# The gate's clamp reads its exponential from PSUM, and four small pieces of the sequence stage change places

## The chip, the cores and the metric

One Trainium2 chip, one of its cores. The metric is the device time of one execution in microseconds (us). The kernel before took 900.95 us, the median of 3 runs (900.33 to 901.28).

## The reference, cut to what matters

32 sequences of 512 tokens with 256 channels each go through an RWKV time-mixing layer with a residual and a layer norm; a second layer then works on a few selected tokens. Only the first layer is touched:

```python
k, v, r = (einsum('btc,oc->bto', x * mix + shifted(x) * (1 - mix), W) for Wk, Wv, Wr)
sr = sigmoid(r)
# per channel, over t:  out = (a + exp(u + k) * v) / (b + exp(u + k))
#                       a = a * ew + exp(k) * v;  b = b * ew + exp(k)
x = layernorm(x + einsum('btc,oc->bto', sr * out, Wo))      # over the 256 channels
```

The second layer (router, top 64 tokens of each pair of half-lengths, attention among them, a feed-forward block, a layer norm) follows when all 32 sequences are through.

## The kernel before, in words

**Tiling.** A sequence is held with its channels on the 128 partitions, in two halves of 512 tokens: a tile of one sequence is 128x1024. The stage over the sequences is a software pipeline written out by hand: each engine has a function `period(at)` that lists what it does in period n, for sequence n and for its neighbours, and `periods` (L367) runs it for 32 periods and DEPTH more, so that the last sequences drain. Nothing else orders the work: each engine executes its list in order and waits on semaphores.

**What each engine does in period n**, in its order:

- TensorE (L640): the three projections of n, K, V and R (L623, 24 matmul instructions in the trace, 8 for each), then the output projection of n-1 with the residual added by a transpose (L635, L637). K waits for `den_done`, V for `num_done` and R for `er_done` of n-1, since those release the PSUM banks.
- ScalarE, ACT in the rows (L932): two exponentials of K of n, one to SBUF and one in place in PSUM (L884, L886); the reciprocal of n-1 as an exponential (L907, waits for `sum_done`); the scaling of the differences of n+1 (L915, three instructions); the exponential of -R (L892, PSUM to the SBUF tile `er`); the logarithm of the denominator (L898, waits for `den_done`); the logarithm of the gate (L902, waits for `clamp_done`); the evacuation of the output of n-1 from PSUM (L923); the rows of n-3, that is the scaling by the layer norm's statistics, four instructions (L928, waits for `nm_done`).
- VectorE, DVE in the rows (L1186): the scan of the denominator of n (L1129, waits for the second exponential of K); the denominator (L1143); the product with V (L1136, in PSUM); the clamp of the gate's exponential to 2^62 (L1149, waits for `er_done`, SBUF to SBUF); the scan of the numerator and the numerator (L1154, L1159); the small shift of n-3 (L1183, 128x4, waits for `s2_done`) and a copy of its statistics (L1184, 128x28); the statistics of n-2: four bn_stats (L1166), four dot products with the router's weights (L1171, a custom instruction with two SBUF inputs of 128x256), four aggregates (L1174) and two small instructions of 128x4 (L1178, L1179).
- GpSimd, POOL in the rows (L558): the difference of n+1 (L525); the gate of n-1, numerator by reciprocal (L547, waits for `rec_done`; its end releases the output projection); three mixes of n+1 (L531, wait for `scaled`); the power for the statistics of n-3 (L554); the sum of the two logarithms of n (L538, waits for `ls_done`).
- SyncE (L468): the loads of sequence n+2 (L456, L457 after `mixed` of n-2 and L461 after `y_ready` of n-2), then the store of n-4 (L466, waits for `rows_done`).

**Buffers.** `er`, `ld`, `den`, `num`, `gg`, `st6`, `stat` and `nm` have two copies each, `xc` and `xt` a ring of four. The PSUM banks of K, V, R and of the output have one copy each.

```python
def statistics_of(s):                       # two SBUF inputs: xt and rwb
    ...
        v.tensor_tensor_reduce(junk[:, j, :], xt[s.k][:, j, :], rwb[:, :], 1.0, 0.0, ALU.mult, ALU.add,
                               stat[par][:, j, 2:3])
```

Of the kernel before, what the change touches and what calls it, by code (L numbers as in the profile page):

```python
# [7 lines left out]
def rwkv_then_selected_block_kernel(nc, x_chan, w_attn, columns, mask_rows, positions,  # L8
# [16 lines left out]
    ALU = mybir.AluOpType  # L25
    ACT = mybir.ActivationFunctionType
# [8 lines left out]
    RING = 4  # L35
# [22 lines left out]
    with ctx:  # L58
# [57 lines left out]
        er = both(CC, T)  # L116
# [31 lines left out]
        psK, psV, psR = ps[:, 0:2, :], ps[:, 2:4, :], ps[:, 4:6, :]  # L148
# [87 lines left out]
        k_ready = sem("k_ready")  # L236
        v_ready = sem("v_ready")
        r_ready = sem("r_ready")
# [5 lines left out]
        er_done = sem("er_done")  # L244
        clamp_done = sem("clamp_done")
# [116 lines left out]

        block = ctx.enter_context(nc.Block())

        DEPTH = 3

        def periods(eng, period):  # L367

# [74 lines left out]
        @block.sync  # L443
        def _(sp):
            sp.dma_start(cols[:, :], columns).then_inc(small_in, 16)
            sp.dma_start(rwb[:, :], router_w.rearrange("(a c) -> a c", a=1).to_broadcast([P, C])).then_inc(small_in, 16)
            sp.dma_start(rbb[:, :], router_b.rearrange("(a c) -> a c", a=1).to_broadcast([P, 1])).then_inc(small_in, 16)

            def load_channels(s):
                if s.had(RING):  # L450

                    sp.wait_ge(mixed, s.n - (RING - 1))
                else:

                    sp.wait_ge(edges_zero, 2 * RING)
                sp.dma_start(xs[s.k][0:HALF, 1:T], x_chan[s.n, 0:HALF, 0:T - 1]).then_inc(chan_in[s.k], 16)  # L456
                sp.dma_start(xs[s.k][HALF:P, 0:T - 1], x_chan[s.n, HALF:P, 1:T]).then_inc(chan_in[s.k], 16)  # L457
                if s.had(RING):

                    sp.wait_ge(y_ready, s.n - (RING - 1))  # L460
                sp.dma_start(xc[s.k][:, :, :], chan_v[s.n]).then_inc(chan_in[s.k], 16)  # L461

            def store_rows(s):

                sp.wait_ge(rows_done, s.n + 1)
                sp.dma_start(out_v[s.n], xt[s.k][:, :, :]).then_inc(row_out[s.k], 16)  # L466

            def period(at):  # L468
                if at.back(-2).exists():
                    load_channels(at.back(-2))  # L470
                if at.had(4) and at.back(4).exists():
                    store_rows(at.back(4))

            load_channels(At(0, 0))
            sp.dma_start(wa[:, :, :, :], w_attn.rearrange("m (c p) o -> p m c o", p=P)).then_inc(w_in, 16)
            load_channels(At(0, 1))
            for k in range(RING):
                period(At(0, k))
            sp.dma_start(ptok[:, :, :], positions.rearrange("p (b j) -> p b j", b=MB)).then_inc(pos_in, 16)
            for dst, src in ((wqk, w_qk), (wv, w_v), (wo, w_o)):  # L480
                sp.dma_start(dst[:, :, :], src.rearrange("(c p) o -> p c o", p=P)).then_inc(w2_in, 16)
            with sp.Fori(1, B // RING - 1) as i:
                for k in range(RING):
                    period(At(i, k))
            for k in range(RING + DEPTH + 1):
                period(At(B // RING - 1, k))

            sp.wait_ge(mall_done, NP)
            sp.wait_ge(ssq_done, NP)
            sp.dma_start(w_stage.rearrange("p (c o) -> p c o", o=F), w_up.rearrange("(c p) o -> p c o", p=P)).then_inc(w_staged, 16)  # L490
            sp.wait_ge(w_split, 1)
            sp.dma_start(w_stage.rearrange("p (c o) -> p c o", o=C), w_down.rearrange("(c p) o -> p c o", p=P)).then_inc(w_staged, 16)
# [113 lines left out]
        def _(pe):  # L606
# [6 lines left out]

            def projections(s):
                pe.wait_ge(mixed, s.n + 1)
                for m, bank, ready, used in ((0, psK, k_ready, den_done), (1, psV, v_ready, num_done), (2, psR, r_ready, er_done)):
                    if s.had(1):

                        pe.wait_ge(used, s.n)
                    for o in range(CC):  # L620
                        for c in range(CC):
                            rhs = xm[s.par][:, m, :] if c == 0 else xc[s.k][:, c, :]
                            last = mm(bank[:, o, :], wa[:, m, c, o * P:(o + 1) * P], rhs, start=(c == 0), stop=(c == CC - 1))  # L623
                    last.then_inc(ready, 1)
# [248 lines left out]
        def _(act):  # L873
            a = nc.scalar
# [12 lines left out]

            def exp_r_of(s):
                act.wait_ge(r_ready, s.n + 1)
                if s.had(2):  # L890
                    act.wait_ge(sum_done, s.n - 1)
                a.activation(er[s.par][:, :, :], psR[:, :, :], ACT.Exp, scale=-1.0).then_inc(er_done, 1)  # L892

            def ln_den_of(s):
                act.wait_ge(den_done, s.n + 1)
                if s.had(2):
                    act.wait_ge(g_ready, s.n - 1)
                a.activation(ld[s.par][:, :, :], den[s.par][:, :, :], ACT.Ln, scale=2.0 ** -DEN_EXP).then_inc(ld_done, 1)  # L898

            def ln_gate_of(s):  # L900
                act.wait_ge(clamp_done, s.n + 1)
                a.activation(er[s.par][:, :, :], er[s.par][:, :, :], ACT.Ln, bias=1.0).then_inc(ls_done, 1)  # L902

            def reciprocal_of(s):

                act.wait_ge(sum_done, s.n + 1)
                a.activation(ld[s.par][:, :, :], ld[s.par][:, :, :], ACT.Exp, scale=-1.0, bias=lnbias[:, 0:1]).then_inc(rec_done, 1)  # L907
# [17 lines left out]
            def rows_of(s):  # L925
                act.wait_ge(nm_done, s.n + 1)
                for j in range(TJ):
                    last = a.activation(xt[s.k][:, j, :], xt[s.k][:, j, :], ACT.Identity,  # L928
                                        scale=stat[s.par][:, j, S2:S2 + 1], bias=nm[s.par][:, j:j + 1])
                last.then_inc(rows_done, 1)  # L930

            def period(at):  # L932
                if at.exists():
                    exp_k_of(at)
                if at.had(1) and at.back(1).exists():
                    reciprocal_of(at.back(1))
                if at.back(-1).exists():
                    differences_scaled(at.back(-1))
                if at.exists():
                    exp_r_of(at)  # L940
                    ln_den_of(at)
                    ln_gate_of(at)
                if at.had(1) and at.back(1).exists():
                    evacuation_of(at.back(1))
                if at.had(3) and at.back(3).exists():
                    rows_of(at.back(3))

            periods(act, period)

# [133 lines left out]
        def _(dve):  # L1083
# [62 lines left out]
            def clamp_of(s):  # L1146

                dve.wait_ge(er_done, s.n + 1)
                v.tensor_scalar(er[s.par][:, :, :], er[s.par][:, :, :], 2.0 ** 62, None, ALU.min).then_inc(clamp_done, 1)  # L1149

            def num_of(s):
                dve.wait_ge(ekv_done, s.n + 1)
# [9 lines left out]
            def statistics_of(s):  # L1162
                par = s.par
                dve.wait_ge(y_read, s.n + 1)
                for j in range(TJ):
                    last = v.bn_stats(st6[par][:, j, :], xt[s.k][:, j, :])  # L1166
                last.then_inc(bn_done, 1)
                for j in range(TJ):
                    if j == TJ - 1:
                        dve.wait_ge(bn_done, s.n + 1)  # L1170
                    v.tensor_tensor_reduce(junk[:, j, :], xt[s.k][:, j, :], rwb[:, :], 1.0, 0.0, ALU.mult, ALU.add,  # L1171
                                           stat[par][:, j, 2:3])
                for j in range(TJ):
                    last = v.bn_aggr(stat[par][:, j, 0:2], st6[par][:, j, :])  # L1174
                last.then_inc(aggr_done, 1)
                dve.wait_ge(aggr_done, s.n + 1)

                v.tensor_scalar(stat[par][:, :, VE], stat[par][:, :, VAR], EPS, None, ALU.add)  # L1178
                v.tensor_scalar(stat[par][:, :, VN], stat[par][:, :, VAR], 1.0 + EPS / 4, EPS * EPS / 4, ALU.mult, ALU.add).then_inc(t2_done, 1)  # L1179
# [6 lines left out]
            def period(at):  # L1186
                if at.exists():
                    den_scan_of(at)
                    den_of(at)
                    products_of(at)  # L1190
                    clamp_of(at)
                    num_of(at)
                if at.had(3) and at.back(3).exists():
                    shift_of(at.back(3))
                if at.had(2) and at.back(2).exists():
                    statistics_of(at.back(2))

            periods(dve, period)

# [290 lines left out]
```

## Time and profile before

| | |
|---|---|
| median of 3 runs | 900.95 us |
| the profiled execution | 907.34 us |
| its span, first to last instruction | 905.6 us |
| granted TensorE clock, mean | 0.942 |
| busy: PE, DVE, ACT, POOL | 779.3, 729.3, 496.5, 437.3 us |
| idle of PE before L635, behind POOL's gate L547 | 27.3 us |
| idle of ACT before its rows L928, behind DVE's shift L1183 | 67.8 us |
| idle of DVE before its scan L1129, behind ACT's L886 | 27.5 us |

The profile shows one execution. A row of the timeline begins with the start and the duration in us, then engine, line, operation, tiles and shapes; "x3" is the number of instructions merged in it, and a bracket gives the idle time of the engine before it and what ended it. Rows of one line give the shortest, the median and the longest duration in ns. Instructions of DVE, ACT and POOL overlap their predecessor a little, so that the step from one start to the next is some 0.04 to 0.1 us shorter than the duration. An instruction that waits for a resource after its start has the wait in its duration.

### The profile page before, as it was taken

How to read it: one execution, taken by the hardware profiler on the slowest of the kernel's cores; microseconds unless marked ns; L12 is line 12 of the kernel's file. 1: busy time of each engine (PE TensorE's matmuls, PEld its weight loads, DVE VectorE, ACT ScalarE, POOL GpSimd, SP SyncE). 2: the span in 40 equal slices, each digit the busy share in tenths (PEclk: the TensorE clock that was granted, in tenths of full speed). 3: DMA queues.
4: the chain of work that ended last, by engine and by line, in shares of the span. 5: the costliest groups of instructions: out<-in, count | busy, mean ns of one | idle time of the engine just before them, and what ended most of it. 6: DMA issues, size and time to landing. Idle time of an engine off the chain costs nothing. (4 is left out here: it accounts for less than half of the span.)

```text
span 905.6 us, 12959 instructions
## 1 busy us (share of the span) xinstructions
PE 779.3 (86%) x4228; PEld 522.4 (58%) x4228; DVE 729.3 (81%) x1505; ACT 496.5 (55%) x825; POOL 437.3 (48%) x303
## 2 busy tenths in 40 slices
PE   7999999999999999999999607397788888799983
PEld 4455554545555554545455405395566666699983
DVE  4689999999999999999999788446777787347773
ACT  2566757676676767676676421063567676431210
POOL 1667686868677786868686505444100000001223
PEclk9999999999999999999999855598999999999996
DMA  7122222231322223221310122342000000000000
GB/s 203 35 82 82 93 82 93 73 100 58 96 78 81 93 81 93 81 93 59 103 58 29 42 70 58 105 117 93 1 2 1 0 1 2 2 1 13 23 24 35
DMA packets 37317, 55.14 MB, mean 61 GB/s; under 512 B 3360, under 2 KB 26528, under 8 KB 37280
## 3 DMA queue, kind: packets, MB, share of 16 engines
q1 hardware_dynamic: 34464, 46.28, 16.4%
q0 software_dynamic: 2816, 8.39, 3.1%
q8 instruction: 21, 0.34, 0.2%
q14 instruction: 16, 0.13, 0.0%
HBM read 35.78 MB, written 18.87 MB: 60 GB/s over the span
## 5 line engine op out<-in xcount | busy, mean ns | idle before, releaser
L623 PE MATMUL ps<-arena,wa 128*128 128x512 f32 x768 | 337.0, 595 | 6.0 <-DMA wa<-w_attn 4.3
L623 PEld LDWEIGHTS ps<-arena,wa 128*128 128x128 f32 x768 | 146.2, 191 | 178.4 <-issue 169.0
L547 POOL TENSOR_TENSOR arena<-arena 128x1024 f32<-128x1024 f32 x32 | 75.5, 2360 | 123.5 <-issue 70.2
L637 PE MATMUL ps<-wa,arena 128*128 128x256 f32 x512 | 133.3, 383 | 0.0
L531 POOL TENSOR_TENSOR arena<-arena 128x512 f32<-128x512 f32 x93 | 128.1, 1407 | 4.6 <-ACT arena L915 4.6
L599 POOL TENSOR_TENSOR fst<-fst,mhalf 128x2 f32<-128x2 f32 x8 | 5.8, 720 | 235.8 <-DVE fst L1448 235.8
L928 ACT ACTIVATE arena<-arena 128x256 f32<-128x256 f32 x128 | 66.3, 590 | 67.8 <-DVE arena L1183 67.8
L1129 DVE TENSOR_TENSOR_SCAN arena<-ewb,ps 128x511 f32<-128x511 f32 x64 | 74.5, 1205 | 27.6 <-ACT ps L886 27.5
L637 PEld LDWEIGHTS ps<-wa,arena 128*128 128x128 f32 x512 | 88.4, 193 | 6.8
L538 POOL TENSOR_TENSOR arena<-arena 128x1024 f32<-128x1024 f32 x32 | 75.1, 2348 | 7.1 <-ACT arena L902 7.1
L635 PE MATMUL ps<-ident,arena 128*128 128x128 f32 x256 | 51.0, 281 | 27.3 <-POOL arena L547 27.3
L1154 DVE TENSOR_TENSOR_SCAN arena<-ewb,ps 128x511 f32<-128x511 f32 x64 | 74.0, 1195 | 0.0
L635 PEld LDWEIGHTS ps<-ident,arena 128*128 128x128 f32 x256 | 34.1, 143 | 62.2 <-POOL arena L547 41.4
L915 ACT ACTIVATE arena<-arena,cols 128x512 f32<-128x512 f32 x93 | 60.0, 710 | 0.0
L902 ACT ACTIVATE arena<-arena 128x1024 f32<-128x1024 f32 x32 | 33.8, 1057 | 46.5 <-DVE arena L1149 46.5
L554 POOL TENSOR_TENSOR arena<-arena,mhalf 128x8 f32<-128x8 f32 x32 | 53.7, 1679 | 7.8 <-DVE arena L1179 7.8
L1149 DVE TENSOR_SCALAR arena<-arena 128x1024 f32<-128x1024 f32 x32 | 51.0, 1594 | 5.0 <-ACT arena L892 4.9
L1078 ACT ACTIVATE arena<-ps 128x512 f32<-128x512 f32 x32 | 19.1, 598 | 61.1 <-PE ps L848 61.1
L859 PE MATMUL ps<-halves 128*128 128x256 f32 x384 | 48.9, 288 | 3.7 <-DVE halves L1419 3.7
L1183 DVE SCALAR_TENSOR_TENSOR arena<-arena 128x4 f32<-128x4 f32 x32 | 44.9, 1402 | 7.4 <-POOL arena L554 7.4
L859 PEld LDWEIGHTS ps<-halves 128*128 128x128 f32 x384 | 48.1, 197 | 3.9 <-DVE halves L1419 3.9
L923 ACT ACTIVATE arena<-ps 128x1024 f32<-128x1024 f32 x32 | 32.7, 1023 | 28.8 <-PE ps L637 28.8
(179 smaller groups left out, 1431.7 us busy)
## 6 DMA issues: line engine op xcount, KB each, us to landing
arena<-x_chan SPq DMA_DIRECT2D x32, 512.0 KB, 3.5
out<-arena SPq DMA_DIRECT2D x32, 512.0 KB, 3.3
arena<-x_chan SPq DMA_DIRECT2D x64, 127.8 KB, 3.2
wa<-w_attn SPq DMA_DIRECT2D x1, 1024.0 KB, 7.9
arena<-w_up SPq DMA_DIRECT2D x1, 1024.0 KB, 4.8
arena<-w_down SPq DMA_DIRECT2D x1, 1024.0 KB, 5.6
wqk<-w_qk SPq DMA_DIRECT2D x1, 512.0 KB, 4.6
wv<-w_v SPq DMA_DIRECT2D x1, 256.0 KB, 5.3
```

Source lines behind the costliest of these rows:

```text
L531: last = g.tensor_tensor(xm[s.par][:, m, :], xm[s.par][:, m, :], xs[s.k][:, :], ALU.add)
L538: g.tensor_tensor(ld[s.par][:, :, :], ld[s.par][:, :, :], er[s.par][:, :, :], ALU.add).then_inc(sum_done, 1)
L547: g.tensor_tensor(gg[s.par][:, :, :], num[s.par][:, :, :], ld[s.par][:, :, :], ALU.mult).then_inc(g_ready, 1)
L554: g.tensor_tensor(stat[s.par][:, :, S1:S2 + 1], stat[s.par][:, :, VE:VN + 1], mhalf[:, 0:2 * TJ].rearrange("p (j a) -> p j a", a=2), ALU.p ...
L623: last = mm(bank[:, o, :], wa[:, m, c, o * P:(o + 1) * P], rhs, start=(c == 0), stop=(c == CC - 1))
L635: mm(psY[:, j, c * P:(c + 1) * P], xc[s.k][:, c, tokens], ident[:, :], is_transpose=True, start=(c == 0), stop=False)
L637: last = mm(psY[:, j, :], gg[s.par][:, c, tokens], wa[:, 3, c, :], start=False, stop=(c == CC - 1))
L859: last = mm(ps[:, 4 + g.par, i * C:(i + 1) * C], x[:, f, i * P:(i + 1) * P], w[:, f, :], start=(f == 0 and t == 0), stop=(f == FC - 1 and ...
L915: last = a.activation(xm[s.par][:, m, :], diff[:, :], ACT.Copy, scale=mix[:, m:m + 1])
L928: last = a.activation(xt[s.k][:, j, :], xt[s.k][:, j, :], ACT.Identity, scale=stat[s.par][:, j, S2:S2 + 1], bias=nm[s.par][:, j:j + 1])
L1129: last = v.tensor_tensor_scan(bb[:, c, 1:T], ewb[:, c, 0:T - 1], psK[:, c, 0:T - 1], 0.0, ALU.mult, ALU.add)
L1154: v.tensor_tensor_scan(aa[:, c, 1:T], ewb[:, c, 0:T - 1], psV[:, c, 0:T - 1], 0.0, ALU.mult, ALU.add).then_inc(scan_a_done, 1)
```

## The change

DEPTH goes from 3 to 4, so every engine has one draining period more; SyncE's list stays as long as it was. ScalarE writes the exponential of -R back to the PSUM bank of R in place of `er`; the clamp reads it there and writes `er`, and now holds the wait on `sum_done` that protects `er`. The R projection of the next sequence waits for `clamp_done` in place of `er_done`. On ScalarE the reciprocal of n-1 comes first in the period, and the rows are those of n-4, between the logarithm of the denominator and that of the gate. On VectorE the small shift and its copy come behind the statistics. The statistics wait for `stats_kept` of two sequences before.

```diff
-        DEPTH = 3
+        DEPTH = 4
...
-            for k in range(RING + DEPTH + 1):
+            for k in range(RING + DEPTH):
                 period(At(B // RING - 1, k))
...
-                for m, bank, ready, used in ((0, psK, k_ready, den_done), (1, psV, v_ready, num_done), (2, psR, r_ready, er_done)):
+                for m, bank, ready, used in ((0, psK, k_ready, den_done), (1, psV, v_ready, num_done), (2, psR, r_ready, clamp_done)):
...
             def exp_r_of(s):
                 act.wait_ge(r_ready, s.n + 1)
-                if s.had(2):
-                    act.wait_ge(sum_done, s.n - 1)
-                a.activation(er[s.par][:, :, :], psR[:, :, :], ACT.Exp, scale=-1.0).then_inc(er_done, 1)
+                a.activation(psR[:, :, :], psR[:, :, :], ACT.Exp, scale=-1.0).then_inc(er_done, 1)
...
             def period(at):
+                if at.had(1) and at.back(1).exists():
+                    reciprocal_of(at.back(1))
                 if at.exists():
                     exp_k_of(at)
-                if at.had(1) and at.back(1).exists():
-                    reciprocal_of(at.back(1))
                 if at.back(-1).exists():
                     differences_scaled(at.back(-1))
                 if at.exists():
                     exp_r_of(at)
                     ln_den_of(at)
+                if at.had(4) and at.back(4).exists():
+                    rows_of(at.back(4))
+                if at.exists():
                     ln_gate_of(at)
                 if at.had(1) and at.back(1).exists():
                     evacuation_of(at.back(1))
-                if at.had(3) and at.back(3).exists():
-                    rows_of(at.back(3))
...
                 dve.wait_ge(er_done, s.n + 1)
-                v.tensor_scalar(er[s.par][:, :, :], er[s.par][:, :, :], 2.0 ** 62, None, ALU.min).then_inc(clamp_done, 1)
+                if s.had(2):
+                    dve.wait_ge(sum_done, s.n - 1)
+                v.tensor_scalar(er[s.par][:, :, :], psR[:, :, :], 2.0 ** 62, None, ALU.min).then_inc(clamp_done, 1)
...
                 dve.wait_ge(y_read, s.n + 1)
+                if s.had(2):
+                    dve.wait_ge(stats_kept, s.n - 1)
...
                     num_of(at)
+                if at.had(2) and at.back(2).exists():
+                    statistics_of(at.back(2))
                 if at.had(3) and at.back(3).exists():
                     shift_of(at.back(3))
-                if at.had(2) and at.back(2).exists():
-                    statistics_of(at.back(2))
```

## Rows read from the trace of the kernel before

**Rows 1.** The page's slices: granted TensorE clock in tenths, 40 slices of the span.
```profile
PEclk9999999999999999999999855598999999999996
```

**Rows 2.** Timeline, PE: the begin of an output projection.
```profile
424.32 0.44 PE L635 MATMUL ps<-ident,arena 128*128 128x128 f32 x2 [0.73 <-POOL arena L547]
```

**Rows 3.** Timeline, DVE and ACT: one round of the closed chain.
```profile
420.74 2.33 DVE L1129 TENSOR_TENSOR_SCAN arena<-ewb,ps 128x511 f32<-128x511 f32 x2 [0.62 <-ACT ps L886]
...
423.17 1.41 DVE L1143 SCALAR_TENSOR_TENSOR arena<-ps,euw,arena 128x512 f32<-128x512 f32 x2
...
425.62 1.65 DVE L1149 TENSOR_SCALAR arena<-arena 128x1024 f32<-128x1024 f32 x1
...
427.20 2.31 DVE L1154 TENSOR_TENSOR_SCAN arena<-ewb,ps 128x511 f32<-128x511 f32 x2
...
430.73 1.62 DVE L1183 SCALAR_TENSOR_TENSOR arena<-arena 128x4 f32<-128x4 f32 x1
...
432.39 2.08 ACT L928 ACTIVATE arena<-arena 128x256 f32<-128x256 f32 x4 [2.46 <-DVE arena L1183]
...
434.38 1.00 ACT L884 ACTIVATE arena<-ps 128x1024 f32<-128x1024 f32 x1
...
436.32 2.33 DVE L1129 TENSOR_TENSOR_SCAN arena<-ewb,ps 128x511 f32<-128x511 f32 x2 [0.62 <-ACT ps L886]
```

**Rows 4.** Timeline, the other steps of the same sequences on ACT and POOL.
```profile
421.91 2.36 POOL L547 TENSOR_TENSOR arena<-arena 128x1024 f32<-128x1024 f32 x1 [3.91 <-issue]
...
424.61 1.06 ACT L898 ACTIVATE arena<-arena 128x1024 f32<-128x1024 f32 x1
...
429.99 2.35 POOL L538 TENSOR_TENSOR arena<-arena 128x1024 f32<-128x1024 f32 x1
...
436.22 1.13 ACT L907 ACTIVATE arena<-arena,lnbias 128x1024 f32<-128x1024 f32 x1
...
437.25 1.94 ACT L915 ACTIVATE arena<-arena,cols 128x512 f32<-128x512 f32 x3
```

**Rows 5.** Timeline, PE: projections of the fourth, the fifth and the last sequence.
```profile
55.61 10.46 PE L623 MATMUL ps<-arena,wa 128*128 128x512 f32 x24
...
70.25 10.46 PE L623 MATMUL ps<-arena,wa 128*128 128x512 f32 x24
...
491.04 10.46 PE L623 MATMUL ps<-arena,wa 128*128 128x512 f32 x24
```

**Rows 6.** By line, POOL's mixes: durations in ns, shortest/median/longest.
```profile
L531 POOL TENSOR_TENSOR arena<-arena x93: 1257/1281/1743, 21.4 to 489.0; 128x512 f32<-128x512 f32 x93
```

**Rows 7.** Timeline: the copy behind the shift and POOL's difference, started together.
```profile
244.75 1.31 DVE L1184 COPY stats_all<-arena 128x28 f32 x1
...
244.75 1.28 POOL L525 TENSOR_TENSOR arena<-arena 128x512 f32<-128x512 f32 x1
```

**Rows 8.** Timeline, second layer: two DVE instructions, two SBUF inputs each, beside POOL.
```profile
619.38 5.95 DVE L1365 TENSOR_TENSOR arena<-arena 128x256 f32<-128x256 f32 x2
...
620.48 4.57 POOL L596 TENSOR_TENSOR halves<-arena,halves 128x2048 fp32r<-128x2048 f32 x1
```

**Rows 9.** By line and timeline, DVE: the dot products and their neighbours.
```profile
L1171 DVE CUSTOM_DVE_ANT_0 arena<-arena,rwb x128: 398/415/422, 59.1 to 523.5; 128x256 f32<-128x256 f32 x128
...
401.12 1.39 DVE L1166 BATCH_NORM_STATS2 arena<-arena 128x6 f32<-128x256 f32 x4
...
402.43 0.40 DVE L1171 CUSTOM_DVE_ANT_0 arena<-arena,rwb 128x256 f32<-128x256 f32 x1
...
404.21 0.17 DVE L1178 TENSOR_SCALAR arena<-arena 128x4 f32<-128x4 f32 x1
```

**Rows 10.** By line, DVE: the product in PSUM, the clamp, the shift.
```profile
L1136 DVE TENSOR_TENSOR ps<-arena,ps x32: 1217/1219/1221, 23.3 to 502.4; 128x1024 f32<-128x1024 f32 x32
...
L1149 DVE TENSOR_SCALAR arena<-arena x32: 686/1670/1817, 25.4 to 503.5; 128x1024 f32<-128x1024 f32 x32
...
L1183 DVE SCALAR_TENSOR_TENSOR arena<-arena x32: 154/1620/1627, 72.4 to 526.2; 128x4 f32<-128x4 f32 x32
```

## The prediction

> **What bounds the kernel now.** I read the slices first, then the timeline of one period in the middle of the sequence stage, then the waits, then the pairs of rows in which VectorE and GpSimd run side by side. The granted clock is at its full 2.4 GHz through the sequence stage [rows 1], so the durations of PE hold for all of it. From the fifth to the last sequence a period takes (491.04 - 70.25) / 27 = 15.58 us [rows 5]. TensorE is nearly full, yet it does not set that length: it waits 0.73 us in each period for the gate [rows 2], and where it does not wait a period is 70.25 - 55.61 = 14.64 us [rows 5]. What sets it is a closed chain of DVE and ACT: scan of the denominator 2.43, denominator and product 2.45, clamp 1.58, scan of the numerator and numerator 3.53, small shift to the rows 1.66, rows to the first exponential 1.99, the two exponentials 1.94, and then the next scan: 15.58 us from start to start [rows 3], the period itself. In that chain both the rows on ACT and the shift on DVE are in line.
>
> Two of its links are long for another reason. The shift of 128x4 takes 154 ns at best and 1620 at the median [rows 10]; it starts at 430.73 and ends at 432.35, when POOL's sum ends (429.99 + 2.35) [rows 3, 4]. The clamp takes 686 ns at best and 1670 at the median [rows 10], beside POOL's mixes, whose own longest is 1743 against a median of 1281 [rows 6]. So a DVE instruction of such a kind waits for the POOL instruction in flight, and holds up the next one. The copy of 128x28 does too: once it started together with POOL's difference and took 1.31 us [rows 7]. Two instructions with two SBUF inputs, one after the other, took 5.95 us from 619.38, to 0.28 us after the end of a POOL instruction of 4.57 us that had started at 620.48 [rows 8]: the second was let in only when that one was over. A waiting DVE instruction gets one turn between two of POOL's, not a run of turns.
>
> **The change part by part.**
>
> *Clamp from PSUM.* No row shows a tensor_scalar of 1024 elements from PSUM. The nearest on the one side is the clamp undisturbed, 0.69 us, on the other the product in PSUM, 1.22 [rows 10]. I take 1.2, since that row too reads 1024 elements from PSUM. Having no second SBUF side, it should no longer wait for the mixes nor delay them: start to start 1.1 in place of 1.58, 0.5 us less on DVE. The exponential written to PSUM costs the same as one to SBUF: ACT's exponential of K writes either, 1.0 us each (the two take 1.94 [rows 3]). The R bank is released later, by the clamp, but R is projected 7.0 us (two thirds of 10.46 [rows 5]) into the period, long after: nothing.
>
> *Shift behind the statistics, rows a sequence later.* It takes shift, rows and exponentials out of line: rows(n-4) find their shift done. Off the old chain go 1.66 + 1.99. On ACT the 1.98 us of rows now stand between the logarithm of the denominator and that of the gate, so gate, sum, reciprocal and gate product come behind them.
>
> *Reciprocal first.* It starts when the sum is over, and no longer behind 1.94 us of exponentials; the exponentials then come 1.0 us behind it.
>
> *The rest.* The store of n-4 is issued behind rows that are done in the middle of the period; behind it on SyncE wait the loads of n+3, needed over a period later, so their cover is some 15 us. The ring of four `xt` still leaves about a period between rows and the next evacuation. The three new waits (stats_kept, and sum_done at the clamp, both two sequences back, and clamp_done) are met long before; behind the clamp's wait on DVE stand the numerator and the statistics. The draining period has no new work. I put 0 on all of this, and 2 us to either side for the drain.
>
> *What the dots meet.* This is the point that decides. Before, the four dots fell into the 3.91 us in which POOL stood idle ahead of its gate [rows 4]; all 128 took 398 to 422 ns [rows 9], so the trace never shows one against POOL. They read two SBUF tensors, as the shift and the pair in [rows 8] do. Cost beside POOL: from 0 (they are a custom instruction and might be free of it) to a whole POOL instruction each. I take the latter. Now the clamp's end is followed by 3.5 us of numerator [rows 3] and 1.3 of bn_stats [rows 9], then the dots; and on POOL the sum 2.35, the difference 1.28 and the gate 2.36 go off one behind the other, since the reciprocal is ready at once. The dots fall among them: one passes after the difference, the second waits out the gate.
>
> Then another chain closes, from the end of the gate to the end of the next. Three dots, aggregates and the two small instructions: four dots and aggregates take 404.21 - 402.43 = 1.78 [rows 9], so 1.4 for three, less 0.1 of overlap; 1.3. The first small tensor_scalar meets the mixes, which start 1.0 + 1.9 + 1.9 + 0.1 = 5.0 us after the start of the reciprocal (that, two exponentials, scaling [rows 3, 4]), the gate 1.3 us after it; so the gate's end is at 3.7 and the mixes begin at 1.3 us behind that, just when it asks. It waits a mix, 1.2; the shift, 0.2 behind it, waits most of the next, 1.1; copy 0.1: den scan at 1.3 + 1.2 + 1.3 = 3.8 us. Scan and denominator 2.43 + 1.41 = 3.85 [rows 3]. ACT: logarithm 1.0, rows 2.0, logarithm 1.06, hand-over 0.1 [rows 3, 4]: 4.15. Sum 2.35, reciprocal 1.13, hand-overs 0.2, gate 2.36 plus 0.1 behind the dot [rows 4]: 6.15. Together 3.8 + 3.85 + 4.15 + 6.15 = 17.95 us in place of 15.58: 2.35 more. PE, at 14.64, then idles some 3.3 us, of which most before V, which waits for the numerator. Here the reordering costs: 2 us of rows stand in the chain, and it contains every POOL step but the mixes.
>
> About 25 periods run at that length (the first six have no dots, or have not drifted yet): 25 x 2.35 = 59 us. On the profiled execution, span 905.6, time 907.34: 966. The profiled execution lies 6.4 us above the median of the runs; carried over to that: 900.95 + 59 = 960 us.
>
> The Trainium skill, SBUF — State Buffer, "Who interferes with whom", says that a Vector instruction with two SBUF inputs contends with a GpSimd instruction that reads SBUF, and that copies and tensor_scalar in a mode that uses both ports do so as well. By that rule the dots and the small tensor_scalar would both wait; the trace agrees for the shift (1620 ns against 154 [rows 10]), and shows no dot beside POOL.
>
> **The rivals.**
>
> *A shorter stall: the small tensor_scalar are free.* If only dots, shift and copy wait, the shift waits the rest of the first mix, 0.9 and no more: the den scan comes at 2.55, the chain is 16.7 us, 25 x 1.1 = 27 us: 928. For it: the race with the mix is a matter of 0.1 us, and no row shows an instruction of 128x4 with one input beside POOL. Against it: clamp and copy, of the same kinds, both wait.
>
> *A longer one.* Where the copy loses its turn as well, as once in 32 [rows 7], a period is 19.1: 25 x 3.5 = 88, 989. I think it rare.
>
> *The other side: the dots do not contend.* Then DVE has 2.43 + 2.45 + 1.1 + 3.53 + 1.3 + 1.78 + 0.2 + 0.2 = 13.0 us of work, and the chain from the denominator's scan through both logarithms, rows, sum, reciprocal and exponentials back to it is 3.85 + 4.15 + 2.4 + 1.1 + 1.95 = 13.45: PE sets the period. 26 x (15.58 - 14.64) = 24, and 1 to 3 us more as the last gate comes earlier: 875. For it: it removes both links that wait now, and the custom instruction is unseen beside POOL. Against: its input count, and the pair in [rows 8]. It decides at the point where a dot beside POOL costs under some 0.4 us.
>
> *No change.* The old rate returns if the dots wait for one POOL instruction in all: 15.6 us, 901.
>
> **How the numbers follow.** 17.95 us a period has 0.36, 16.7 has 0.32, 19.1 has 0.08; the dots free 0.19; no change 0.05. The predicted time is that of the first, 960. The slower cases run from 928 (less 10 for a later onset and the clamp's lower bound, so 915) to 989: that is 0.76; down to 901 takes in no change: 0.81. The range is 900 to 990 and leaves out the dots free. Faster or slower count from 0.2%, 1.8 us, about what a measurement of this kernel can tell from no change: 0.19 faster, 0.05 the same, 0.76 slower.
>
> **What would show it.** Right: the dots' longest at 2 us or more in place of 422 ns; the first small tensor_scalar at 1.2 us; the clamp at a steady 1.2, mixes at 1.28; PE idle before its projections behind DVE's numerator; a period near 18 us. Dots at 0.4 us beside POOL and a period of 14.64 would make it wrong on the other side; tensor_scalar at 0.17 with dots that wait give 16.7. If the clamp still swings with the mixes, my first term is wrong.

## The result, and the profile after

The changed kernel takes 957.19 us, the median of 4 runs (954.4 to 959.73), against 900.64 us for the one before: a ratio of 1.063, 95% interval 1.0588 to 1.0672. It is slower by 6.3%; the forecast was 960 us.

The page of the changed kernel, part 2 (TensorE's busy tenths and its granted clock) and part 5 (groups by line; behind the bar the busy time, the mean of one in ns, and the engine's idle time ahead of them with what ended most of it):

```profile
PE   7999888888889888888888861688688889799983
...
PEclk9999999999999999999999976559799999999996
...
L623 PE MATMUL ps<-arena,wa 128*128 128x512 f32 x768 | 355.3, 615 | 66.7 <-DVE arena L1160 49.2
...
L1174 DVE CUSTOM_DVE_ANT_0 arena<-arena,rwb 128x256 f32<-128x256 f32 x128 | 126.6, 1041 | 0.0
...
L896 ACT ACTIVATE arena<-arena 128x1024 f32<-128x1024 f32 x32 | 33.8, 1056 | 89.5 <-DVE arena L1142 89.5
...
L926 ACT ACTIVATE arena<-arena 128x256 f32<-128x256 f32 x128 | 65.9, 586 | 5.1 <-DVE arena L1186 5.1
```

In these tenths the clock of the sequence stage is as before [rows 1]. Taken period by period it is not quite: in 6 of the last 25 periods TensorE's clock falls to its lower level, 1.2 GHz, for some 3 us (granted clock 0.50 from 124.60 to 127.10, 0.91 over that period), where the kernel before has 1.00 in every one. It costs no more than the last period's 0.9 us: a period with such a fall takes 18.7 us and the one behind it 16.9, together two of 17.8, and e8 below has the same period without one fall. The time lies in the waits. TensorE now waits 66.7 us ahead of its projections, 49.2 of them for VectorE's numerator (L1160). The wait of ACT's rows for the shift, 67.8 us in the table of before, is 5.1: the change did cut that link. In its place the dot products, 0.41 us each before, take 1.04 on average.

PE's timeline in the changed kernel gives the period. A row of 24 matmul instructions holds the projections of K, V and R; where V waits, the 8 of K stand apart. The row at 123.47 is V and R with a fall of the clock in it:

```profile
85.30 10.46 PE L623 MATMUL ps<-arena,wa 128*128 128x512 f32 x24
...
99.98 3.67 PE L623 MATMUL ps<-arena,wa 128*128 128x512 f32 x8
105.69 7.13 PE L623 MATMUL ps<-arena,wa 128*128 128x512 f32 x16 [2.03 <-DVE arena L1160]
...
117.77 3.67 PE L623 MATMUL ps<-arena,wa 128*128 128x512 f32 x8 [0.61 <-DVE arena L1142]
123.47 8.83 PE L623 MATMUL ps<-arena,wa 128*128 128x512 f32 x16 [2.03 <-DVE arena L1160]
...
545.92 3.60 PE L623 MATMUL ps<-arena,wa 128*128 128x512 f32 x8
```

From 85.30 to 99.98 PE still sets the period, 14.68 us. Then comes a step to 17.79, and from 99.98 to the last sequence 25 periods take (545.92 - 99.98) / 25 = 17.84 us, against 15.58 [rows 5]. That is 25 x 2.26 = 56 us, as much as the medians are apart. The two traces say nearly the same: the last sequence begins 545.92 - 491.04 = 54.9 us later.

The new closed chain, called the ring below, runs from the end of one gate to the end of the next. One round of it, from the timeline of DVE, ACT and POOL in the changed kernel:

```profile
410.30 2.41 POOL L547 TENSOR_TENSOR arena<-arena 128x1024 f32<-128x1024 f32 x1
...
410.44 2.56 DVE L1174 CUSTOM_DVE_ANT_0 arena<-arena,rwb 128x256 f32<-128x256 f32 x1
...
413.93 3.73 POOL L531 TENSOR_TENSOR arena<-arena 128x512 f32<-128x512 f32 x3 [1.22 <-ACT arena L913]
414.02 1.20 DVE L1181 TENSOR_SCALAR arena<-arena 128x4 f32<-128x4 f32 x1
...
415.21 1.23 DVE L1186 SCALAR_TENSOR_TENSOR arena<-arena 128x4 f32<-128x4 f32 x1
...
416.45 2.31 DVE L1128 TENSOR_TENSOR_SCAN arena<-ewb,ps 128x511 f32<-128x511 f32 x2
...
418.87 1.41 DVE L1142 SCALAR_TENSOR_TENSOR arena<-ps,euw,arena 128x512 f32<-128x512 f32 x2
...
420.31 1.06 ACT L896 ACTIVATE arena<-arena 128x1024 f32<-128x1024 f32 x1 [3.79 <-DVE arena L1142]
...
421.27 2.06 ACT L926 ACTIVATE arena<-arena 128x256 f32<-128x256 f32 x4
...
423.24 1.04 ACT L900 ACTIVATE arena<-arena 128x1024 f32<-128x1024 f32 x1
...
424.42 2.35 POOL L538 TENSOR_TENSOR arena<-arena 128x1024 f32<-128x1024 f32 x1 [5.15 <-ACT arena L900]
...
426.73 1.27 POOL L525 TENSOR_TENSOR arena<-arena 128x512 f32<-128x512 f32 x1
...
427.30 0.99 DVE L1174 CUSTOM_DVE_ANT_0 arena<-arena,rwb 128x256 f32<-128x256 f32 x1
...
428.18 2.35 POOL L547 TENSOR_TENSOR arena<-arena 128x1024 f32<-128x1024 f32 x1 [0.18 <-ACT arena L905]
```

The gate ends at 412.71, and the second dot, started at 410.44, ends 0.29 us behind it. The first small tensor_scalar starts 0.09 us behind the first mix and lasts 1.20; the shift lasts 1.23 beside the second mix. The scan of the denominator follows 3.74 us behind the gate's end. From there it is 3.86 us to the logarithm of the denominator (L896), 4.11 us with the rows and the logarithm of the gate (L900) to the sum, and 6.11 us to the end of the next gate (430.53): 17.82 us. The first dot of the next round (427.30) lasts 0.99: it ends 0.29 us behind POOL's difference, which ends at 428.00.

By line, the clamp, the first small tensor_scalar and the mixes of the changed kernel (shortest/median/longest in ns):

```profile
L1150 DVE TENSOR_SCALAR arena<-ps x32: 1215/1217/1225, 25.3 to 561.0; 128x1024 f32<-128x1024 f32 x32
...
L1181 DVE TENSOR_SCALAR arena<-arena x32: 171/1178/1203, 62.8 to 581.3; 128x4 f32<-128x4 f32 x32
...
L531 POOL TENSOR_TENSOR arena<-arena x93: 1260/1267/1284, 21.3 to 541.0; 128x512 f32<-128x512 f32 x93
```

### The profile page after: what moved, and what is told of

Its sections match the earlier page's. It is cut to its first block and busy times, and to the rows that moved or that the text cites. A ratio compares the mean times of both kernels' runs of the same rounds, so it can differ in the third digit from the quotient of the medians.

```text
span 958.0 us, 12995 instructions
## 1 busy us (share of the span) xinstructions
PE 796.7 (83%) x4228; PEld 527.0 (55%) x4228; DVE 810.4 (85%) x1505; ACT 492.9 (51%) x825; POOL 427.2 (45%) x303
## 3 DMA queue, kind: packets, MB, share of 16 engines
q1 hardware_dynamic: 34464, 46.28, 15.8%
## 5 line engine op out<-in xcount | busy, mean ns | idle before, releaser
L623 PE MATMUL ps<-arena,wa 128*128 128x512 f32 x768 | 355.3, 615 | 66.7 <-DVE arena L1160 49.2
L531 POOL TENSOR_TENSOR arena<-arena 128x512 f32<-128x512 f32 x93 | 115.5, 1269 | 42.8 <-ACT arena L913 42.8
L1174 DVE CUSTOM_DVE_ANT_0 arena<-arena,rwb 128x256 f32<-128x256 f32 x128 | 126.6, 1041 | 0.0
L896 ACT ACTIVATE arena<-arena 128x1024 f32<-128x1024 f32 x32 | 33.8, 1056 | 89.5 <-DVE arena L1142 89.5
L890 ACT ACTIVATE ps<-ps 128x1024 f32<-128x1024 f32 x32 | 32.3, 1008 | 71.7 <-PE ps L623 71.7
L905 ACT ACTIVATE arena<-arena,lnbias 128x1024 f32<-128x1024 f32 x32 | 36.8, 1149 | 49.8 <-POOL arena L538 49.8
L554 POOL TENSOR_TENSOR arena<-arena,mhalf 128x8 f32<-128x8 f32 x32 | 52.7, 1648 | 9.0 <-DVE arena L1182 9.0
L635 PEld LDWEIGHTS ps<-ident,arena 128*128 128x128 f32 x256 | 36.5, 143 | 34.9 <-issue 16.7
L859 PEld LDWEIGHTS ps<-halves 128*128 128x128 f32 x384 | 49.2, 202 | 3.9 <-DVE halves L1422 3.9
```

The source lines that it names most:

```text
L531: last = g.tensor_tensor(xm[s.par][:, m, :], xm[s.par][:, m, :], xs[s.k][:, :], ALU.add)
L635: mm(psY[:, j, c * P:(c + 1) * P], xc[s.k][:, c, tokens], ident[:, :], is_transpose=True, start=(c == 0), stop=False)
L859: last = mm(ps[:, 4 + g.par, i * C:(i + 1) * C], x[:, f, i * P:(i + 1) * P], w[:, f, :], start=(f == 0 and t == 0), stop=(f == FC - 1 and ...
```

## The experiments

Two theories stood against each other. **A**: the ring is closed by VectorE's instructions that wait out POOL's, above all the dots behind the gate. **B**: only the work put in line counts (2 us of rows between the two logarithms); waits beside POOL don't matter. The kernels are called e1 to e10. The first four kernels and the ninth and tenth ran where the kernel before takes 901 us; the fifth to the eighth where it takes 910.92, so the ratio to before is what compares.

| kernel | median us | before | ratio, 95% interval |
|---|---|---|---|
| the changed kernel | 957.19 | 900.64 | 1.063 (1.0588 to 1.0672) |
| e1 changed, reciprocal back | 876.32 | 901.2 | 0.9726 (0.9682 to 0.9769) |
| e2 changed, rows at the end | 918.12 | 901.2 | 1.0189 (1.0146 to 1.0233) |
| e3 changed, shift first | 925.55 | 901.2 | 1.0272 (1.0209 to 1.0334) |
| e4 changed, dots with one input | 875.65 | 901.2 | 0.9718 (0.9679 to 0.9758) |
| e5 before, rows later | 891.49 | 910.92 | 0.9789 (0.9738 to 0.9839) |
| e6 before, clamp from PSUM | 902.05 | 910.92 | 0.9899 (0.9843 to 0.9956) |
| e7 before, reciprocal first | 898.09 | 910.92 | 0.9861 (0.9832 to 0.989) |
| e8 changed, clamp in SBUF | 969.23 | 910.92 | 1.0642 (1.0611 to 1.0673) |
| e9 changed, small instructions as memsets | 926.03 | 901.56 | 1.0273 (1.0252 to 1.0294) |
| e10 as e1, three rounds | 874.13 | 901.56 | 0.9707 (0.9683 to 0.9732) |

### The reciprocal put back

```diff
             def period(at):
-                if at.had(1) and at.back(1).exists():
-                    reciprocal_of(at.back(1))
                 if at.exists():
                     exp_k_of(at)
+                if at.had(1) and at.back(1).exists():
+                    reciprocal_of(at.back(1))
```

> The changed kernel with the reciprocal put back behind the two exponentials of K; all else as changed. Theory A (a ring closed by the dots that wait out POOL's gate): the gate now starts some 1.9 us later after the sum, so the four dots, the small instructions and the shift find POOL with only its difference to do and pass before the gate; the ring opens and PE sets the period at 14.64 us, 25 to 27 periods x 3.15 us less than the 957 us of the changed kernel: about 875 us, dots at 0.4 us (one of four up to 1 us). Theory B (the length is only that of the work put in line, the 2 us of rows between the two logarithms; no wait for a port matters): the rows still stand there and nothing gets shorter, 955 to 960 us.

Measured: 876.32 us, the ratio 0.9726. A holds, B does not: the same work on every engine, with one instruction 1.9 us later, takes 81 us less than the changed kernel. PE's timeline of this kernel:

```profile
394.08 10.46 PE L623 MATMUL ps<-arena,wa 128*128 128x512 f32 x24
...
408.72 10.46 PE L623 MATMUL ps<-arena,wa 128*128 128x512 f32 x24
```

The period is 14.64 us, the one without waits [rows 5]. And what the dots meet, on DVE and POOL:

```profile
426.24 0.63 DVE L1174 CUSTOM_DVE_ANT_0 arena<-arena,rwb 128x256 f32<-128x256 f32 x1
...
426.54 1.46 POOL L525 TENSOR_TENSOR arena<-arena 128x512 f32<-128x512 f32 x1
...
426.81 1.48 DVE L1174 CUSTOM_DVE_ANT_0 arena<-arena,rwb 128x256 f32<-128x256 f32 x1
...
429.54 0.17 DVE L1187 COPY stats_all<-arena 128x28 f32 x1
...
430.11 2.37 POOL L547 TENSOR_TENSOR arena<-arena 128x1024 f32<-128x1024 f32 x1 [2.11 <-issue]
```

The dots still wait, for the end of the sum and for the difference, but all of them and the copy behind them (429.54) are through before the gate begins at 430.11.

### The dots with one input

```diff
-                    v.tensor_tensor_reduce(junk[:, j, :], xt[s.k][:, j, :], rwb[:, :], 1.0, 0.0, ALU.mult, ALU.add,
-                                           stat[par][:, j, 2:3])
+                    v.bn_stats(junk[:, j, 0:6], xt[s.k][:, j, :])
```

> The changed kernel with each of the four dot products replaced by a bn_stats of the same 128x256 (one SBUF input, 0.33 us in place of 0.35), so that VectorE has the same work but none of the four takes a second SBUF input; the dot product with the router's weights is left out and the selection goes by the mean in its place. Theory A: without the dots' wait the ring is not closed, the small instructions come long before the mixes, and PE sets the period: 14.64 us, about 875 us. Theory B: the same work in the same places, 957 us.

Measured: 875.65 us. By line, the durations in ns (shortest/median/longest) of the four replacements in this kernel:

```profile
L1176 DVE BATCH_NORM_STATS2 arena<-arena x128: 405/409/416, 58.9 to 496.9; 128x6 f32<-128x256 f32 x128
```

and of the dots in the changed kernel:

```profile
L1174 DVE CUSTOM_DVE_ANT_0 arena<-arena,rwb x128: 405/418/2595, 58.9 to 580.5; 128x256 f32<-128x256 f32 x128
```

The reciprocal is still first and the rows are still between the logarithms; only the four dots are replaced, and the whole loss is gone. This is the direct test of the step that decides: the loss hangs on the dots and their waits for POOL. That a dot waits because of its second SBUF input is not separated here, since bn_stats is another operation and writes 6 elements in place of 256 as well. The Trainium skill (SBUF — State Buffer, "Who interferes with whom") says that a Vector instruction with two SBUF inputs contends with a GpSimd instruction that reads SBUF. The trace agrees for the dots: 0.41 us alone, up to 2.6 behind a gate.

One wait did not go. The first small tensor_scalar of this kernel now asks during the gate and waits that out, longer than in the changed kernel:

```profile
412.26 1.93 DVE L1182 TENSOR_SCALAR arena<-arena 128x4 f32<-128x4 f32 x1
...
414.34 2.31 DVE L1130 TENSOR_TENSOR_SCAN arena<-ewb,ps 128x511 f32<-128x511 f32 x2
```

POOL's gate ends at 414.16, and the scan starts 0.18 us behind it, where 3.74 us lay between the two in the changed kernel. So, by an estimate from the legs of the changed kernel, a ring of 17.82 - 3.74 + 0.18 = 14.3 us is left. That is under TensorE's 14.64, and the wait costs nothing.

### The other moves undone, one at a time

The rows at the end of ACT's period:

```diff
-                if at.had(4) and at.back(4).exists():
-                    rows_of(at.back(4))
-                if at.exists():
                     ln_gate_of(at)
                 if at.had(1) and at.back(1).exists():
                     evacuation_of(at.back(1))
+                if at.had(4) and at.back(4).exists():
+                    rows_of(at.back(4))
```

> The changed kernel with the rows (still those of four sequences back) at the end of ACT's period. Theory A: the ring loses 1.98 us of rows but the dots still wait out the gate; the small instructions then meet the mixes at another point; worked through step by step a period of about 16.3 us, 957 - 25 x 1.5 = about 918 us (910 to 925), with dots still up to 2.5 us. Theory B: the 2 us of rows go fully, 25 x 2 = 50 us less, 907 us, and with nothing else in line the period falls on towards 14.64 (875).

Measured: 918.12 us, and a period of 422.40 - 406.23 = 16.17 us in PE's timeline:

```profile
406.23 3.60 PE L623 MATMUL ps<-arena,wa 128*128 128x512 f32 x8
411.10 7.13 PE L623 MATMUL ps<-arena,wa 128*128 128x512 f32 x16 [1.27 <-DVE arena L1159]
...
422.40 3.60 PE L623 MATMUL ps<-arena,wa 128*128 128x512 f32 x8
```

The ring loses 1.65 us and stays closed: its dots last up to 2.58 us. B, by which the period had to fall to 15.8 or below, falls here too. But the 1.65 us do not come from the moved rows alone. Four lines of one round:

```profile
405.36 1.06 ACT L896 ACTIVATE arena<-arena 128x1024 f32<-128x1024 f32 x1 [2.25 <-DVE arena L1141]
...
407.54 1.06 ACT L900 ACTIVATE arena<-arena 128x1024 f32<-128x1024 f32 x1 [1.13 <-DVE arena L1149]
...
412.73 2.50 POOL L547 TENSOR_TENSOR arena<-arena 128x1024 f32<-128x1024 f32 x1 [0.40 <-ACT arena L905]
...
416.19 0.17 DVE L1180 TENSOR_SCALAR arena<-arena 128x4 f32<-128x4 f32 x1
```

With nothing between the two logarithms, the logarithm of the gate waits 1.13 us for the clamp (L1149), so logarithm to sum (408.74) takes 3.38 us in place of 4.11: only 0.73 less. The leg from the gate's end to the scan (415.23 to 417.59) is 1.38 shorter: one dot fewer is left behind the gate, and the first small tensor_scalar therefore comes just ahead of the first mix and lasts 0.17. The other two legs are 0.08 and 0.38 longer.

The shift first:

```diff
+                if at.had(3) and at.back(3).exists():
+                    shift_of(at.back(3))
                 if at.had(2) and at.back(2).exists():
                     statistics_of(at.back(2))
-                if at.had(3) and at.back(3).exists():
-                    shift_of(at.back(3))
```

> The changed kernel with the small shift and its copy put back ahead of the statistics. Theory A: the shift waits out a part of the sum again, but no longer behind the dots, where it met the second mix; the ring through gate and dots loses that one wait: about 16.7 us a period, 957 - 25 x 1.1 = about 929 us. Theory B: the shift is not in line with anything after the change, no difference: 957 us.

Measured: 925.55 us. The placing of the shift behind the statistics alone costs 957.19 - 925.55 = 32 us, 1.3 us in each of 25 periods. Shift and copy stand for 1.24 us of the ring above (415.21 to 416.45), nearly all of it the shift's wait for a mix.

The two small instructions as memsets:

```diff
-                v.tensor_scalar(stat[par][:, :, VE], stat[par][:, :, VAR], EPS, None, ALU.add)
-                v.tensor_scalar(stat[par][:, :, VN], stat[par][:, :, VAR], 1.0 + EPS / 4, EPS * EPS / 4, ALU.mult, ALU.add).then_inc(t2_done, 1)
+                v.memset(stat[par][:, :, VE], 1.0)
+                v.memset(stat[par][:, :, VN], 1.0).then_inc(t2_done, 1)
```

> The changed kernel with the two small tensor_scalar of 128x4 behind the aggregates replaced by memsets of the same 128x4, which read nothing from SBUF; the variance is left out of the layer norm's scale (a constant stands there). Theory A (each of the waits counts by itself): the first small instruction no longer waits 1.2 us for the first mix; the shift takes that wait over, 0.9 to 1.1 us, and the second mix is met by nobody: 16.7 us a period, ratio to before about 1.03, 928 us. Rival (all the waits of the ring fall to the dots and the shift alone): no difference, ratio 1.063, 957 us.

Measured: 926.03 us, ratio 1.0273, and 430.43 - 413.88 = 16.55 us a period in PE's timeline:

```profile
413.88 3.60 PE L623 MATMUL ps<-arena,wa 128*128 128x512 f32 x8
419.12 7.13 PE L623 MATMUL ps<-arena,wa 128*128 128x512 f32 x16 [1.65 <-DVE arena L1160]
...
430.43 3.60 PE L623 MATMUL ps<-arena,wa 128*128 128x512 f32 x8
```

This is the case of the prediction's first rival, brought about: with small instructions that are free of POOL the ring is 16.7 us long by its count and 16.55 by the trace. So the wait of a 128x4 tensor_scalar is a term of its own, worth 31 us.

The clamp in SBUF again (the exponential of R to `er`, as before):

```diff
-                a.activation(psR[:, :, :], psR[:, :, :], ACT.Exp, scale=-1.0).then_inc(er_done, 1)
+                if s.had(2):
+                    act.wait_ge(sum_done, s.n - 1)
+                a.activation(er[s.par][:, :, :], psR[:, :, :], ACT.Exp, scale=-1.0).then_inc(er_done, 1)
...
-                v.tensor_scalar(er[s.par][:, :, :], psR[:, :, :], 2.0 ** 62, None, ALU.min).then_inc(clamp_done, 1)
+                v.tensor_scalar(er[s.par][:, :, :], er[s.par][:, :, :], 2.0 ** 62, None, ALU.min).then_inc(clamp_done, 1)
```

> The changed kernel with the clamp part undone (exponential of R to SBUF, clamp there). Theory A: the clamp is not in the new ring (it comes behind the denominator, beside ACT's logarithm and rows), so the period stays near 17.8 us: 955 to 958 us. If the clamp's place or the later release of the R bank mattered, the time would fall by 25 x 0.5 us or more, to 945 us or under.

Measured: ratio 1.0642 against 1.063: no difference. The clamp itself went from a steady 1.22 us to 0.69 us, since in the new order it comes when POOL stands idle:

```profile
L1150 DVE TENSOR_SCALAR arena<-arena x32: 684/686/1064, 26.4 to 559.5; 128x1024 f32<-128x1024 f32 x32
```

So in the new order reading PSUM makes the clamp dearer by half a microsecond. That costs nothing, for the clamp is not in the ring there. TensorE's clock stays at its upper level through all the periods of e8, which take 17.80 us, so the falls of the clock in the changed kernel do not make its period.

### Each part alone, on the kernel before

Rows a sequence later, at their old place:

```diff
-        DEPTH = 3
+        DEPTH = 4
...
-                if at.had(3) and at.back(3).exists():
-                    rows_of(at.back(3))
+                if at.had(4) and at.back(4).exists():
+                    rows_of(at.back(4))
```

> The kernel before with one part of the change alone: the rows are those of four sequences back, at the same place at the end of ACT's period (DEPTH 4). Theory A: the chain shift, rows, exponentials, scan that set the 15.58 us is cut, since the rows no longer wait for this period's shift; the gate comes behind the exponentials, so the dots keep their gap on POOL: PE sets the period at 14.64 us, about 877 us. Theory B (work in line on ACT is what counts): the rows still stand ahead of the exponentials, same time, 900 us.

Measured: ratio 0.9789, where 877 us would be 0.973, just under the interval; the period is 14.64 us as expected:

```profile
406.35 10.46 PE L623 MATMUL ps<-arena,wa 128*128 128x512 f32 x24
...
420.99 10.46 PE L623 MATMUL ps<-arena,wa 128*128 128x512 f32 x24
```

The old chain is cut by this one part. Some 4 us of the expected gain are missing, and they do not lie in the sequence stage: its last sequence starts at 464.90, 26.1 us earlier than in the trace of before (491.04). Behind that start e5 takes 423.0 us, e6, e7 and e8 421.0 to 423.4, the trace of before 414.6 and e1 408.0. So all four traces from that chip are slower in this part; no profile of the kernel before was taken there, and the two runs of e5 are 3.7 us apart, so the 4 us stay open. The clamp still lasts 1.8 us beside the mixes, and it costs nothing now.

The clamp from PSUM alone (the edit above, the other way round):

> The kernel before with the clamp part of the change alone (exponential of R in PSUM, clamp reads it there). Theory A: the clamp, in line in the old chain, costs 1.1 us start to start in place of 1.58: 15.58 - 0.47 = 15.1 us a period, about 888 us. If the clamp's wait for the mixes was hidden, no difference: 900 us.

Measured: ratio 0.9899, 892 us on the scale of 901. PE's projections are 418.29 - 403.15 = 15.14 us apart in its timeline, where 15.1 was expected:

```profile
403.15 10.46 PE L623 MATMUL ps<-arena,wa 128*128 128x512 f32 x24
...
418.29 10.46 PE L623 MATMUL ps<-arena,wa 128*128 128x512 f32 x24
```

The number came out, but not by the count that was expected. The clamp takes 1.14 us start to start (415.62 to 416.76), 0.44 less than before, and the way from the shift's start to the rows is shorter too, 1.30 us (405.08 to 406.38) in place of 1.66. Together that is more than the 0.44 by which the period fell. In its place the copy behind the shift now waits out POOL's difference, in 27 of 32 sequences:

```profile
405.08 1.27 DVE L1183 SCALAR_TENSOR_TENSOR arena<-arena 128x4 f32<-128x4 f32 x1
406.27 1.32 DVE L1184 COPY stats_all<-arena 128x28 f32 x1
...
410.75 2.32 DVE L1127 TENSOR_TENSOR_SCAN arena<-ewb,ps 128x511 f32<-128x511 f32 x2
```

The scan starts at 410.75 with no idle time of VectorE ahead of it, 0.48 us behind the end of the exponential (410.27) for which it waited before. So in most periods of e6 VectorE's own list, with its waits, sets the period.

The reciprocal first alone:

> The kernel before with the reciprocal first on ACT alone. Theory A: the rows still end the period, so the exponentials of K come 1.04 us later behind rows and reciprocal, and the gate earlier; the dots begin to meet the gate: worked through, 14.7 to 15.2 us a period after a long start, about 888 us (880 to 905), the dots partly above 0.42 us. A plain reading of the chain (1.04 us more in line): 16.6 us, 925 us.

Measured: ratio 0.9861, 888 us on that scale. The period is 429.23 - 414.18 = 15.05 us:

```profile
414.18 10.88 PE L623 MATMUL ps<-arena,wa 128*128 128x512 f32 x24
...
429.23 10.87 PE L623 MATMUL ps<-arena,wa 128*128 128x512 f32 x24
```

The plain reading, 1.04 us more in line and so 16.6 us, fails. With the gate and mixes at other points the clamp lasts 1.31 us and the shift 0.39, where they had 1.65 and 1.62 [rows 3]: 1.57 us less against 1.04 more, and the period falls by 0.53. The expected meeting of dots and gate did not come about: the dots' mean is 429 ns, and one of 128 waited, 2.56 us.

### The version that is faster than both

> The changed kernel with the reciprocal back behind the exponentials again, timed in three rounds: the version that is faster than both. Theory A: PE sets every period from the fourth on, ratio to before 0.972, within 0.003. If the first measurement rested on a chance order of dots and gate, the ratio lies above 0.98 here.

Measured: 874.13 us, median of 4 runs, ratio 0.9707, interval 0.9683 to 0.9732. All parts of the change but the reciprocal's place make a kernel 27 us faster than the one before. e4 comes as low, but without the dot products; what e1, e4, e5 and e10 share is PE's own 14.64 us a period, which no move of these parts can undercut.

## Why the prediction was right

**What bounded the kernel before.** The closed chain of shift, rows and exponentials was the bound: e5 cuts it at the rows, and PE sets the period. e6 is weaker support than its number suggests: two links get shorter by 0.8 us together, the period falls by 0.44, and another path, VectorE's own list, holds it there.

**Clamp.** 1.2 us taken, 1.22 measured, steady; mixes at 1.27 with 1.28 as the longest, where 1.74 was the longest before [rows 6]. Against the clamp of before that is the 0.5 us less that was forecast. Against a clamp in SBUF in the new order it is 0.5 us more (e8), and neither counts in the new ring.

**What the dots meet.** "One passes after the difference, the second waits out the gate" is what 427.30 and 410.44 show, and e4 shows it to be the cause: without the dots the loss is gone. Whether it is their second SBUF input, as the prediction has it, is argued from the rule and not shown apart.

**The ring.** Forecast 3.8 + 3.85 + 4.15 + 6.15 = 17.95 us, measured 3.74 + 3.86 + 4.11 + 6.11 = 17.82. No term is off by more than 0.06; their sum, with 25 periods, gave 59 us where 56 were measured. In one place the forecast had luck. Its count puts the question of the first small tensor_scalar and the begin of the mixes both at 1.3 us behind the gate's end, a tie, and takes the wait. Measured, the mix begins at 1.22 and the tensor_scalar asks at 1.31, and in 26 rounds the mix is ahead by 0.09 to 0.13 us. The count could not decide that; e9 gives its price, 31 us, and in e2 it went the other way.

**Nothing for the rest.** DEPTH, the stores, the new waits: e1 has all of them and runs at PE's rate, so together they cost nothing that shows.

**The rivals.** The dots do contend (e4), so the kernel that would have been faster is not this one; but the forecast for that case, 875 us, is what e4 and e1 measured. The shorter stall, 928 us, came out as e9 at 926. The longer one, by the copy's wait, did not occur in the changed kernel, whose copy lasts 176 ns at most; e6 shows that it is not rare everywhere.

What the prediction did not say, though its own count holds it: the loss hung on one place in one list. With the reciprocal 1.9 us later the dots fit between sum and gate. The prediction named the reciprocal's place as a cause of the gate's early start, but gave the cost of the reordering first to the 2 us of rows in line. Moving the rows away (e2) gives back 39 us, and by the legs of its ring less than half of that, 0.73 of 1.65 us a period, comes from the rows; putting the reciprocal back (e1) gives back all, 81 us.

## What to carry to other kernels

Where VectorE and GpSimd work on SBUF side by side, a timeline must be read for what an instruction meets, not only for the semaphore it waits for. In this kernel the instructions with two SBUF inputs, the copy and the tensor_scalar within SBUF waited out the GpSimd instruction in flight (0.41 us became 2.6, 0.17 became 1.2), and back-to-back ones got one turn between two of GpSimd's. Such a wait costs only where it is in line: 1.93 us cost nothing in e4, 1.2 us cost 31 us in the changed kernel. Before an instruction is moved forward, look for the gap that its lateness leaves: here the idle time of POOL ahead of its gate was the slot in which the dots ran. And count a moved step in the closed ring of one period, with these waits in it; the sum over an engine's work does not show the bound (VectorE's went from 729.3 us, 81% of the span, to 810.4, 85%, though it had no more to do).

## What the runs showed that was not expected

- An instruction of 16 bytes a partition can cost 31 us. The first tensor_scalar of 128x4, 0.17 us alone, lasts 1.18 us at the median in the changed kernel. Its input and output have a stride of 7 elements, and it waits all the same. What it costs hangs on 0.1 us: in e2 it comes just ahead of the mix and lasts 0.17.
- A kernel can get faster when a step is put in line (e7), since its neighbours then meet other instructions of POOL. And a forecast can be right in its number by another path (e6).
- Not every POOL instruction holds VectorE up for all of its time. In the kernel before one power of 128x8 (L554, start 502.12) lasted 2.14 us in place of 1.65, and the clamp that began beside it at 503.53 took its undisturbed 0.69: there it was POOL that waited. In e7 the power lasts 2.10 us in nearly every period, beside a clamp that started ahead of it. No run was made on this.
